# Scores of a group's first tile ahead of its query projection instead of behind it

## The reference

```
for i in range(6):
    x = attn_layer(shift_tokens(x), Wqkv[i], q_scale[i], k_scale[i], Wo[i]) + x
    x = ffn_layer(shift_tokens(x), ln_g[i], ln_b[i], W1[i], b1[i], W2[i], b2[i]) + x

# attn_layer
q, k, v = split(x @ Wqkv)                 # 16 heads of 64
q, k = l2norm(q) * qs, l2norm(k) * ksc    # then rotary: q * cos + rotate_half(q) * sin, k alike
sim = einsum('bhwie,bhwje->bhwij', q, k) * 8.0      # the scores, masked to j <= i
out = einsum('bhwij,bhwje->bhwie', softmax(sim), v) # the values' product
return out @ Wo
# ffn_layer
xn = (x - mu) / sqrt(var + 1e-05) * g + bln
a, gate = split(xn @ W1 + b1)
return a * gelu(gate) @ W2 + b2
```

## Time and profile before

| | us |
|---|---|
| median of three runs | 2850.4 (2847.1 to 2854.09) |
| the profiled execution | 2847.98 |
| its span | 2846.2 |
| its mean granted clock of TensorE | 0.988 of full |

### The profile page before, as it was taken

The page is one execution under the profiler, slowest core; times in us unless marked ns, Lnnn a source line. Parts: engine busy times, 40 slices in busy tenths (PEclk is TensorE's granted clock), DMA queues, the critical chain, the costliest instruction groups (busy, mean ns, idle before and its releaser), DMA issues.

```text
span 2846.2 us, 92826 instructions
## 1 busy us (share of the span) xinstructions
PE 2691.9 (95%) x36416; PEld 2060.1 (72%) x36417; DVE 2600.1 (91%) x3375; ACT 2246.7 (79%) x3776; POOL 2116.7 (74%) x1529
## 2 busy tenths in 40 slices
PE   8799978999999999999999999999999999999996
PEld 7577756777777777777777777777777777777774
DVE  7899968999999999999999999999999999999993
ACT  5799957878788787878888787888878787887873
POOL 6766658777778777778777787777787777877771
PEclk9899999999999999999999999999999999999998
DMA  1000013232223332223232232222322322322222
GB/s 57 24 2 2 1 35 76 67 76 69 67 69 75 73 73 66 69 71 75 66 79 69 66 75 71 72 67 70 76 67 68 79 62 68 72 67 58 64 66 79
DMA packets 103719, 178.41 MB, mean 63 GB/s; under 512 B 29350, under 2 KB 52708, under 8 KB 103396
## 3 DMA queue, kind: packets, MB, share of 16 engines
q1 hardware_dynamic: 102372, 174.60, 25.2%
q10 hardware_dynamic: 1152, 1.20, 0.1%
HBM read 22.62 MB, written 2.10 MB: 9 GB/s over the span
## 4 chain that ended last, share of the span: by engine, by line
PE 30%; POOL 16%; issue 15%; ACT 11%; DMA 7%; DVE 5%; SPq 1%; POOLq 0%; ACTq 0%; DVEq 0%
PE pa L843 9%; POOL spare L1446 8%; DMA kT<-spare 7%; PE px L872 5%; PE pg L982 3%; PE ps L903 3%; PE pg L960 3%; PE px L917 3%; PE pg L974 2%; POOL xs_lo L1432 2%; DVE ss L1269 2%; ACT spare L1095 2%; POOL pr L1484 2%; ACT spare L1041 1%; POOL spare L1455 1%
## 5 line engine op out<-in xcount | busy, mean ns | idle before, releaser
L1446 POOL TENSOR_TENSOR spare<-spare,qk_t 128x1024 f32<-128x1024 f32 x384 | 910.1, 2392 | 10.9 <-POOL xs_lo L1432 8.1
L843 PE MATMUL pa<-w_hi,xs_hi 128*128 128x512 f32 x1152 | 511.9, 444 | 25.3 <-issue 8.6
L1462 POOL TENSOR_TENSOR sm<-sm,inv 128x512 f32<-128x512 f32 x192 | 201.8, 1051 | 429.2 <-DVE sm L1307 361.4
L1285 DVE TENSOR_TENSOR qk_t<-pa,rot 128x1024 f32<-128x1024 f32 x384 | 464.6, 1210 | 1.6 <-ACT spare L1048 0.8
L1276 DVE TENSOR_TENSOR spare<-pa,rot 128x1024 f32<-128x1024 f32 x384 | 464.6, 1210 | 0.0
L1269 DVE TENSOR_REDUCE ss<-spare 128x16 f32<-128x1024 f32 x384 | 457.7, 1192 | 6.1 <-ACT spare L1041 5.2
L843 PE MATMUL pa<-w_hi,xs_lo 128*128 128x512 f32 x1152 | 459.2, 399 | 0.3 <-DMA pT<-prT 0.3
L843 PE MATMUL pa<-w_lo,xs_hi 128*128 128x512 f32 x1152 | 455.0, 395 | 0.0
L872 PE MATMUL px<-ident_sb,spare 128*128 128x128 f32 x3072 | 407.2, 276 | 18.8 <-POOL spare L1455 11.9
L1455 POOL TENSOR_TENSOR spare<-spare,inv 128x1024 f32<-128x1024 f32 x192 | 365.9, 1905 | 69.6 <-ACT inv L1080 65.3
L872 PEld LDWEIGHTS px<-ident_sb,spare 128*128 128x128 f32 x3072 | 340.4, 140 | 105.1 <-issue 44.6
(11 more groups left out here) (178 smaller groups left out, 5926.1 us busy)
## 6 DMA issues: line engine op xcount, KB each, us to landing
kT<-spare SPq DMA_DIRECT2D x384, 256.0 KB, 3.7
pT<-prT SPq DMA_DIRECT2D x768, 64.0 KB, 2.0
w_part<-in_Wqkv SPq DMA_DIRECT2D x40, 192.0 KB, 3.7
wo<-in_Wo SPq DMA_DIRECT2D x6, 512.0 KB, 5.5
c_h<-in_x SPq DMA_DIRECT2D x4, 512.0 KB, 9.5
spare<-in_x SPq DMA_DIRECT2D x8, 256.0 KB, 4.8
out<-spare SPq DMA_DIRECT2D x8, 256.0 KB, 2.5
wo<-in_W SPq DMA_DIRECT2D x6, 341.0 KB, 5.2
```

Of the source, the lines that this page charges most:

```text
L843: last = pe.matmul(pa[(u + c) % 2][:, half * 512:half * 512 + 512], x[:, j * P:(j + 1) * P], w[:, at], start=(k == 0), stop=(k == 2))
L1285: dve.tensor_tensor(halves(qk_t[:, c, :]), halves(pa[(3 * j + c) % 2][:])[:, :, ::-1, :], table.unsqueeze(1).to_broadcast([P, HEADS, 2, DH ...
L1446: pool.tensor_tensor(qk_r[:, c, :], qk_r[:, c, :], qk_t[:, c, :], ALU.add)\
```

## The change

A constant `SCORES_FIRST = (0,)` names the tiles `j` of a group whose scores TensorE issues ahead of the query projection. All other tiles keep their order. Only TensorE's program is touched.

```diff
         HALF_TOK = 2 * P
+        SCORES_FIRST = (0,)
...
                     for j in range(GT):
                         if j == 2:
                             a_block(i, 2, 0)
+                        if j in SCORES_FIRST:
+                            scores(i, j, 2)
                         project_q(i, j, l)
                         if j == 2:
                             a_block(i, 2, 1)
-                        scores(i, j, 2)
+                        if j not in SCORES_FIRST:
+                            scores(i, j, 2)
                         if j == 0:
                             subtract_mean(i, 2)
                         transpose_q(i, j, 1)
```

## The result

| | us |
|---|---|
| median after (5 runs) | 2864.66 (2862.45 to 2866.64) |
| median before (5 runs by then) | 2850.4 (2847.1 to 2854.09) |
| ratio, 95% interval | 1.0047 (1.0032 to 1.0062) |
| the profiled execution after, its span | 2865.85, 2864.1 |

The kernel became slower by 14.3 us, 0.5%. 2865 was forecast.

What follows compares the result with a forecast made beforehand. No busy share decides; TensorE has no room for three quarters of a group. Terms 5.4 + 4.7 + 5 = 15.1 us on 2848.0 gave 2863, with the median's 2.4 more 2865; range 2850 to 2878, forecast's own 2857 to 2877.

Steps and rivals of the forecast that it cites:

- The scores and the landing: First tile: scores lose the projection as cover, start at 0.45 instead of 1.83 us; 0.18 is new waiting for keys.
- VectorE's gain counted at nothing: First tile's maximum: its 0.45 us wait goes, but GpSimd's product of the probabilities hides all but 0.02.
- 0.45 a group would be gained: First tile, VectorE: the gain claimed if GpSimd's product of the probabilities ended early.
- ScalarE's 0.18: First tile: late projection delays ScalarE's centred square from 4.10 to 4.28 us, and everything to the gelu by 0.18.
- The gelu has no cover: Second tile: gate block's weights load at 17.30 instead of 17.12 us, costing 0.18 in each of 30 loop groups, 5.4 us.
- Late landings: First tiles whose keys' second half lands late, formerly behind the projection, now show: together 5 us.
- Written-out groups and first turns: One written-out group and one first loop turn of each layer, 11 in all, lose 0.43 each: 4.7 us.
- The rounding groups: Six written-out groups where ScalarE first rounds the output weights, so the square of q starts late anyway: lose nothing.
- It is absorbed: Rival, chance 0.24: ScalarE catches up between 4.28 and 17 us, the loop's 5.4 us vanish; 2856 us.
- It gets faster: Rival, chance 0.07: VectorE's 0.45 us at the first tile's maximum is gained over 47 groups, 21 us; 2829 us.
- it loses more: Rival, chance 0.09: projection follows scores slowly and scores wait at the loop head; 32 us lost, 2882 us.
- The upper prices of the prediction: High ends without a row: scores behind the loop head +3, scores to projection +14 us, landings 7 instead of 5.

Runs made afterwards that it cites:

- experiment 1: Second half of the keys of each group's first tile cut to 4 of 64 rows: changed kernel 2851.19 us, kernel before 2854.12 us.
- experiment 7: Keys' transposes in the fourth tile moved behind a quarter of the output projection: changed kernel 2853.18 us, kernel before 2853.01; a third version added inverse norms first.
- experiment 5: Changed kernel with GpSimd's product of the probabilities cut to one of 16 heads for the tile in question: 2862.82 us.
- experiment 2: Changed kernel with ScalarE's inverse norms ahead of the square of q in a group's first tile: 2861.46 us.
- experiment 3: Changed kernel with the first tile's scores between the two halves of the query projection: 2858.61 us.
- experiment 4: Changed kernel with the swap made in each group's fourth tile instead of its first: 2877.09 us.
- the last of 7: Changed kernel with the keys' transposes earlier in the fourth tile and inverse norms ahead of the square of q in the first: 2855.36 us.
- experiment 6: Second half of every tile's keys issued by ScalarE instead of SyncE: changed kernel 2917.13 us, kernel before 2891.89 us.

## Why the prediction was right, and where its sizes were not

**The scores and the landing**: right in every row, and experiments 1 and 7 show that it is the cause.

**VectorE's gain counted at nothing**: right. The reason given was half of it, as experiment 5 shows: with the product early the gain would have been held by the late square of q, and "0.45 a group would be gained" was wrong.

**ScalarE's 0.18**: right in size (0.22 at the centred square, 0.19 at the gelu, 0.18 at the gate block's weights), and experiment 2 shows that it is the carrier in quiet loop groups.

**"The gelu has no cover"**: this step failed, and with it the term of 5.4 us, 0.18 in each of 30 groups; 0.09 a group was measured. I read the earlier trace rows as the start of the block and took 0.18 from there to the group's length. The weight loads run ahead of the products. Before, the sample's products:

```profile
1497.55 0.40 PE L843 MATMUL pa<-w_hi,xs_lo 128*128 128x512 f32 x1
1497.78 0.40 PE L960 MATMUL pg<-fn_hi,w_hi 128*128 128x512 f32 x1
```

After, the weights:

```profile
1503.19 0.19 PEld L961 LDWEIGHTS pg<-fn_hi,w_hi 128*128 128x128 f32 x1 [0.18 <-ACT gt L1130]
```

and the product they were loaded for:

```profile
1503.05 0.40 PE L844 MATMUL pa<-w_hi,xs_lo 128*128 128x512 f32 x1
1503.29 0.40 PE L961 MATMUL pg<-fn_hi,w_hi 128*128 128x512 f32 x1
```

Before, the products stood 0.23 behind their weights, because the projection ahead of them was still running. After, they stand 0.10 behind. So the block had a cover of about 0.12, and of the 0.24 in the sample 0.11 reached the products (they start at 17.46 instead of 17.35). As medians the weights are 0.18 late, the products 0.05, the groups 0.09 longer. Forecast was 0.18 each. I had looked at the engine's queue and not at the instruction that it feeds.

The products' 0.05 is not what sets the 0.09, though. The keys' transposes that follow them wait for ScalarE's copy of q, which stands behind the gelu. Before:

```profile
1497.39 1.01 ACT L1088 COPY qT<-px 128x1024 f32<-128x1024 f32 x1
```

```profile
1498.54 1.06 PE L872 MATMUL px<-ident_sb,spare 128*128 128x128 f32 x8
```

After:

```profile
1503.03 1.01 ACT L1092 COPY qT<-px 128x1024 f32<-128x1024 f32 x1
```

```profile
1504.18 1.06 PE L873 MATMUL px<-ident_sb,spare 128*128 128x128 f32 x8
```

The transposes start 0.14 to 0.15 behind the end of that copy in all 30 loop groups of both kernels, so ScalarE's lateness passes there whole: 18.31 instead of 18.11 as medians. Behind them TensorE makes up about half: the gate block's third part is 0.13 late, the values' product 0.09, and it stays at 0.09 to the group's end. What takes off this second part was not tested.

**Late landings**, 5 us forecast: right in kind, about right in size. The worst sample is the first loop turn whose values' product ended at 1286.06 after the change. TensorE and ScalarE of after there:

```profile
1287.70 1.10 PE L904 MATMUL ps<-kT,qT 128*32 128x64 f32 x64 [1.64 <-DMA kT<-spare]
```

```profile
1290.43 1.02 ACT L1045 ACTIVATE spare<-pa 128x1024 f32<-128x1024 f32 x1 [1.82 <-PE pa L844]
```

The keys land 1.59 behind that end, 1.60 in before, where the scores started at 1.64 as well, behind the projection and without a wait. Now the projection comes 2.7 later than it did, and the group has 51.15 us instead of 49.17. A late landing passes into the length with little taken off: in the latest of the later turns the scores start at 1.69, 1.42 behind the loop head's 0.27, and the group is 1.34 longer. The 30 loop groups grow by 5.17 us together: six with a late landing by about 3.4 of it, the other 24 by about 0.07 each. The forecast had 5.4 for the quiet part, which came to 1.8.

**Written-out groups and first turns**, 0.43 each forecast: as medians 0.49 in the five written-out ones and 0.78 in the six first turns, where late landings are among them (8.0 us together instead of 4.7). **The rounding groups**, nothing forecast: -0.05 each. These groups vary from run to run, though. In the two variants of the kernel before, whose loop groups are as long as its own, they add up to 3.7 and 6.5 us more than in the kernel before. The medians of the loop groups are firm to 0.02, the sums over the 17 others to some 5 us.

**The sum.** The profiled execution is 17.9 us longer than before's: 12.1 in the groups, 0.5 ahead of them, 5.3 behind the last group. The forecast for the groups was 15.1. The 5.3 are in no term, and nothing shows that they are of the change: four kernels that have it (experiments 1, 2, 3 and 7) end as the kernel before does. Behind the last group both kernels do the same work at different granted clocks. One stretch of low clock from each follows (they are not the same piece of the work). Before, the columns being us, busy time of PE, PEld, DVE, ACT and POOL, clock, DMA:

```profile
2809.00:2817.00 8.00, 8.00 (x32) 6.42 (x32) 0.70 (x2) 0.00 (x0) 0.00 (x0) 0.79 0.24 63
```

After:

```profile
2825.60:2834.00 8.40, 8.39 (x25) 6.62 (x26) 0.00 (x0) 0.00 (x0) 0.00 (x0) 0.65 0.01 3
```

The mean clock of this tail is 0.82 in one and 0.73 in the other. It comes out as the one or the other in the profiled executions of experiments 1 to 5 and 7, whatever the edit: 72.3 to 73.0 us of tail at 0.82 and more in six of them and in the kernel before, 76.3 to 77.9 at 0.74 and less in the changed kernel and in those of experiments 4, 5 and the last of 7. Each kernel was profiled once, so this tells two executions apart and not two kernels. The timed runs show as much: the kernel before alone has mean granted clocks from 0.984 to 0.990 in the 29 runs beside experiment 7, and times from 2846.2 to 2860.32, the longer ones mostly at the lower clocks. What sets the clock stays open. The forecast of 2865 and the 2864.66 agree partly by luck: the groups lost 3 us less than the 15.1, and the forecast was built on a median of 2850.4, 1.2 to 1.6 below those of the 73 later runs. Of the 14.3 between the medians, how much is the tail can't be said.

**The rivals.** "It is absorbed" was half right: about half of the loop's 0.18 is absorbed, on TensorE in the second tile and not on ScalarE. "It gets faster" and "it loses more" did not happen: the step from scores to projection took 1.03, the low end. (The upper prices of the prediction, 3 + 14 + 2 us, add up to 2884 and not to the 2877 given as the upper end.) The rule of the Trainium skill's "Perfetto Trace Analysis", section "Identifying the Most-Contended Engine", judges TensorE's headroom by the weight loads' share (78% in that stretch), and read so it would have given the first rival. It did not tell whether a delay is absorbed: in experiment 4 a new wait of 0.39 in that stretch made the group 0.30 longer.

## What to carry to other kernels

When work is moved ahead of other work on one engine, ask what the other work was covering. Here the query projection covered a transfer's landing, and the half microsecond that VectorE was seen to wait for the scores was worth nothing, since two other things ended at nearly the same time. Follow a delay past the weights' load to the product that consumes it, and from there to the next instruction that waits for the same engine: here the two came 0.05 and 0.20 late. And judge a wait by the idle time that it adds to what was there before, not by its size.

## What the runs showed of the hardware

- Two transfers of 256 KB issued together ended when they ended with the second issued 0.54 later: 3.17 and 4.26 us after the first issue in both cases (medians of 192 pairs).
- An issue of a transfer on ScalarE's queue cost ScalarE 0.57 us of standing still (experiment 6, median of 192).
- In the last 72 to 78 us the granted clock was about 0.82 or about 0.73 from one profiled execution to the next, for about 5 us of the time, with the same work.
- The transposes that waited for ScalarE's copy of q started 0.14 to 0.15 us behind its end, in all 30 loop groups before and after.
- The loop's head cost TensorE 0.26 to 0.27 us whatever stood behind it, projection or scores, unless a transfer's landing was later and covered it.
